# A causal layer's inverse products, split by token halves over two row halves of TensorE's array

## The chip, the cores and the metric

The kernel runs on one core of a Trainium2 chip. The metric is the device time of one execution in microseconds; the time given for a kernel is the median of its runs. A profiled execution gives, beside its own time, the trace: every instruction on the five engines (PE is TensorE with PEld its weight loads, DVE is VectorE, ACT is ScalarE, POOL is GpSimd, SP is SyncE, which issues DMAs), with its start, its duration and what it waited for.

## The reference

A model of four layers over x of 4 sequences x 512 tokens x 128 channels: a state space layer, an attention block with routed experts, a causal layer, and the attention block again. The change lies in the third, the causal layer:

```python
probs = jax.nn.softmax(logits + causal_mask, axis=-1)      # 16 heads of 8 channels, rotary q and k
L = jnp.eye(s, dtype=probs.dtype) - jnp.tril(probs, -1)
rhs = jnp.diagonal(probs, axis1=-2, axis2=-1)[..., None] * v
A = jax.scipy.linalg.solve_triangular(L, rhs, lower=True)
attn_output = A.transpose(0, 2, 1, 3).reshape(b, s, HID)
return attn_output @ Wd.T + bd
```

So each token's row is its own probability times v plus a weighted sum of the solved rows of all earlier tokens: a triangular solve for each head.

## The kernel before

`delta_phase` computes the causal layer. Tokens go in 16 tiles of 128 (4 a sequence, `n` counts them), and each tile in 8 blocks of 16 tokens (`BLK`, `BLKS`). E is the matrix of exponentials of a tile's own scores, kept for each head in `e_nat` (tokens x earlier tokens); `xT` holds, for each head, the inverses of the eight 16 x 16 diagonal blocks, scaled by the row sums, and zeros elsewhere. POOL makes the inverses (`inverse_block`), and SyncE brings them into place by DMA (`inverses`).

`multiplied` on TensorE makes the inverse products: for every head one matmul with `e_nat` as the stationary and `xT` as the moving operand, 128 x 128 x 128 in f32, four heads in one PSUM bank (L2560), and `multiplied` on ScalarE copies the bank of 128 x 512 into `mT` (L2146). There are four such groups a tile, at the hooks 9, 10, 11 and 12 (`MT_HOOKS`) of the tile before. PSUM has eight banks: two for step sums (`STEP`), two for transposes (`TURN`), two that ScalarE empties (`TO_ACT`) and two that VectorE empties (`TO_DVE`). Uses of `TO_ACT` are numbered in program order by `act_use`; they alternate between the two banks, and `act_free` makes TensorE wait until the use two before has been copied out.

The solve of a tile then takes 7 steps (k = 1 to 7, `TURNS` is the last), for two halves of 8 heads that take turns. A half step is: `product` on TensorE (L2601), for 8 heads, two rounds of four heads side by side in strips of 32 columns, with `a_nat`'s first 16k tokens as the stationary operand and 16 columns of `mT` as the moving one; an addition by VectorE into `aT` (L2430); `turned` on TensorE, a transpose of all 128 tokens of `aT` (`turn_half`, L2606), where `aT` is the stationary operand and the identity the moving one; a copy by ScalarE into `a_nat`, or after the last step into `a_all` (`turned`, L2183). Steps 1 to 7 of both halves make 14 hooks, and `beside(n, h)` puts other tiles' work between them, in an order written out by hand: maxima of tile n+4 or n+3, scores of n+3 (`score`), sums and their transposes of n+2, inverse products of n+1. At a tile's start come the products with earlier tiles (`from_earlier`), transposes of `gT`, and the first product with `xT` (`inverse`). Every engine runs its own queue in program order.

Of the kernel before, what the change touches and what calls it, by code (L numbers as in the profile page):

```python
# [19 lines left out]
P = 128  # L20
# [1707 lines left out]
def delta_phase(core, nc):  # L1728
# [4 lines left out]
    with ExitStack() as ctx:  # L1733
# [64 lines left out]
        def shift_in(n):  # L1798
            return s["m_in_odd" if n % 2 else "m_in_even"]

        def later_tiles(n):
            b, t = bt(n)
            return b * (TPB - 1) + t
# [10 lines left out]
        def own_cols(t, half):  # L1814

            n = NH // 2 * HEAD_COLS
            pairs = t[:, half * n:(half + 1) * n + 2 * HD].rearrange("p (g r) -> p g r", g=2)
            return pairs[:, :, 0:n // 2].rearrange("p g (h c) -> p g h c", h=GROUP)[:, :, :, 0:HD]
# [7 lines left out]
        def turn_bank(half):  # L1826
            return ps[:, TURN[half], 0:P]

        def turned_cols(half):
            return turn_bank(half).rearrange("p (h c) -> p h c", h=GROUP)[:, :, 0:2 * HD].rearrange(  # L1830
                "p h (g d) -> p g h d", g=2)

        def in_program(n):
# [62 lines left out]
        def act_use(kind, n, i=0):  # L1896
            act_place[kind, n, i] = len(act_place)
# [4 lines left out]
        for n in range(-LEAD, TILES_N):  # L1902
            if n >= 1:
                dve_use("output", n - 1)
            for h in range(HOOKS):
                if in_program(n + 2) and (n + 2) % TPB and h == 2:
                    dve_use("turned_sums", n + 2)
                if starts_in(n, 4) is not None and h == 6:
                    dve_use("own", starts_in(n, 4))
                if maxima_done(n, h) is not None:  # L1910
                    dve_use("turned_maxima", maxima_done(n, h))
                for m, hd in maxima_in(n, h):
                    dve_use("maximum", m, hd)
                if starts_in(n, LEAD) is not None and h == 13:
                    dve_use("values", starts_in(n, LEAD))
                if begins_early(n + 1) and h == 13:
                    dve_use("first_tiles", n + 1)
                for i in scores_in(n, h):
                    act_use("score", n + 3, i)
                if in_program(n + 1) and h in MT_HOOKS:  # L1920
                    act_use("mt", n + 1, MT_HOOKS.index(h))
                if in_program(n + 2) and (n + 2) % TPB and h == 0:
                    act_use("sums", n + 2)
                if in_program(n + 2) and h == 3:
                    act_use("column", n + 2)
                if goes_on(n, LEAD) is not None and h == 12:
                    act_use("hT", goes_on(n, LEAD))
                if goes_on(n, 5) is not None and h in (0, 1):
                    act_use("qk", goes_on(n, 5), h)
        dve_use("output", TILES_N - 1)  # L1930

        def in_act(kind, n, i=0):
            return act_place[kind, n, i] + 1
# [4 lines left out]
        def act_bank(kind, n, i=0):  # L1938
            return ps[:, TO_ACT[act_place[kind, n, i] % 2], :]
# [8 lines left out]
            return in_act("score", n, DIAG_GROUPS - 1)  # L1948

        def all_mt(n):  # L1950
            return in_act("mt", n, len(MT_HOOKS) - 1)

        def all_maxima(n):
            return in_dve("maximum", n, NH // heads_at_once(n) - 1)
# [5 lines left out]
        with nc.Block() as block:  # L1960
# [129 lines left out]
            def _(act):  # L2090
# [51 lines left out]
                                             bank[:, 0:heads * t * P], ACT.Exp, scale=SCALE).then_inc(s["act_out"], 1)  # L2142

                def multiplied(n, i):
                    act.wait_ge(s["act_ps"], in_act("mt", n, i))
                    nc.scalar.copy(mT[:, n % 2, i * GROUP:(i + 1) * GROUP, :].rearrange("p h i -> p (h i)"),  # L2146
                                   act_bank("mt", n, i)).then_inc(s["act_out"], 1)

                def sums_leave(n):
                    act.wait_ge(s["act_ps"], in_act("sums", n))  # L2150
# [28 lines left out]

                def turned(n, half, k):  # L2180
                    act.wait_ge(s["an_ps"], 2 * (n * BLKS + k) + half + 1)
                    out = a_all[:, n % TPB, :] if k == TURNS else a_nat[:, :]
                    nc.scalar.copy(own_cols(out, half), turned_cols(half)).then_inc(s["an_sb"], 1)  # L2183

                act.wait_ge(s["set"], 5)
                for n in range(-LEAD, TILES_N):
# [259 lines left out]
            def _(pe):  # L2446
# [107 lines left out]
                def multiplied(n, i):  # L2554
                    if i == 0:
                        pe.wait_ge(s["x_in"], 16 * BLKS * (n + 1))
                    bank = act_free("mt", n, i)
                    for hh in range(GROUP):
                        hd = i * GROUP + hh
                        last = nc.tensor.matmul(bank[:, hh * P:(hh + 1) * P], e_nat[:, n % 3, hd, :], xT[:, n % 2, hd, :],  # L2560
                                                start=True, stop=True)
                    last.then_inc(s["act_ps"], 1)

                def head(half, gl, hh):
                    return (2 * half + gl) * GROUP + hh
# [36 lines left out]
                                                    of_head(lhs[rows, :], hd), rhs(hd), start=(gl == 0), stop=(gl == 1))  # L2602
                    last.then_inc(done, 1)

                def turn_half(half, src, done):
                    nc.tensor.transpose(turn_bank(half), src[:, half, :], core.ident[:, :]).then_inc(done, 1)  # L2606

                def output(n):
                    bank = dve_free("output", n)
# [37 lines left out]
                def turned(n, half, k):  # L2647
                    pe.wait_ge(s["at_sb"], 2 * (n * BLKS + k) + half + 1)
                    if n >= 1 and k == 0:
                        pe.wait_ge(s["an_sb"], 2 * BLKS * n - 1 + half)  # L2650
                    turn_half(half, aT[:, n % 2], s["an_ps"])

                pe.wait_ge(s["set"], 5)
                for n in range(-LEAD, TILES_N):
# [114 lines left out]
```

## Time and profile before

| | us |
|---|---|
| median of three runs (lowest, highest) | 1573.53 (1573.26, 1580.44) |
| the profiled execution | 1573.51 |
| its span, first to last instruction | 1571.7 |
| TensorE busy | 1268.3 (81%) |
| VectorE busy | 996.3 (63%) |
| ScalarE busy | 726.2 (46%) |
| GpSimd busy | 626.5 (40%) |
| mean granted clock of TensorE | 0.849 |

Busy time counts an engine's instructions; a share of the whole span mixes layers with different limits, so it has to be read stage by stage. TensorE's granted clock is given as a share of 2.4 GHz: it stands either at 1.00 (2.4 GHz) or at 0.50 (1.2 GHz), and a mean in between is a mixture of both.

### The profile page before, as it was taken

Reading aid. Unit: us, or ns where it says so; the run is one execution under the profiler, and the core shown is the slowest. Engines: PE = TensorE matmul, PEld = TensorE weight load, DVE = VectorE, ACT = ScalarE, POOL = GpSimd, SP = SyncE. Lnnn points to the kernel's source line nnn. Section 1 sums busy time; section 2 is a strip of 40 time slices with the busy share of each in tenths; the row PEclk is TensorE's granted clock in tenths of the full one; section 3 lists DMA queues with packets and bytes.
Section 4 is the critical chain, followed back from the end, with each engine's and each line's share of the span. In section 5 each row is a group of like instructions: output and inputs, shape, how many; then the busy total and the mean of one; then the engine's idle time right before and its main releaser. Section 6 shows DMA issues by size and latency. Waiting matters only on the chain. (4 is left out here: it accounts for less than half of the span.)

```text
span 1571.7 us, 30564 instructions
## 1 busy us (share of the span) xinstructions
PE 1268.3 (81%) x11629; PEld 698.6 (44%) x11658; DVE 996.3 (63%) x2122; ACT 726.2 (46%) x1578; POOL 626.5 (40%) x838
## 2 busy tenths in 40 slices
PE   7857677689999949237889999988989799999765
PEld 3323233233333329124766666666666223333365
DVE  3699999788879435336546646645522777887143
ACT  3833344217777827113524523623442057777543
POOL 1388898653241225203423333333231712522143
PEclk9988888869999979656779879978977579999878
DMA  4379742131431102131331231141120333140122
GB/s 136 147 255 377 266 155 86 49 84 34 114 75 48 69 24 62 35 81 23 64 51 28 46 68 30 34 82 19 27 38 9 79 68 70 55 110 22 56 64 76
DMA packets 127270, 126.36 MB, mean 80 GB/s; under 512 B 86802, under 2 KB 111954, under 8 KB 121525
## 3 DMA queue, kind: packets, MB, share of 16 engines
q1 hardware_dynamic: 123822, 118.28, 27.3%
q0 software_dynamic: 2496, 5.13, 1.1%
q8 instruction: 93, 1.52, 0.4%
q10 hardware_dynamic: 806, 0.99, 0.2%
q14 instruction: 53, 0.43, 0.1%
HBM read 103.56 MB, written 38.62 MB: 90 GB/s over the span
## 5 line engine op out<-in xcount | busy, mean ns | idle before, releaser
L1280 DVE TENSOR_REDUCE f_row_min<-f_ps 128x1 f32<-128x512 f32 x512 | 324.2, 679 | 73.3 <-PE f_ps L1557 69.6
L1188 ACT ACTIVATE f_e<-f_ps 128x512 f32<-128x512 f32 x512 | 280.4, 602 | 147.9 <-PE f_ps L1577 142.2
L1557 PE MATMUL f_ps<-f_operands 72*128 72x512 bf16 x512 | 212.1, 425 | 28.7 <-DMA f_operands<-k_scr 14.9
L1577 PE MATMUL f_ps<-f_operands 75*128 75x512 bf16 x512 | 190.3, 387 | 6.0 <-DMA f_operands<-m_scr 3.4
L738 PE MATMUL m_ps<-m_shared,sb_ident 128*128 128x512 f32 x256 | 137.1, 684 | 53.7 <-DVE m_shared L594 52.3
L357 POOL TENSOR_TENSOR m_drive<-m_du,m_ring 128x1024 f32<-128x1024 f32 x64 | 151.0, 2375 | 52.4 <-DVE m_ps L586 33.2
L474 ACT ACTIVATE m_ps<-m_delta,m_A 128x511 f32<-128x511 f32 x128 | 83.1, 681 | 129.3 <-DVE m_ps L586 104.7
L1588 PE MATMUL f_ps<-f_e,f_v_op 128*32 128x512 f32 x1024 | 138.2, 611 | 2.4 <-ACT f_e L1188 1.4
L2278 DVE TENSOR_REDUCE d_row_min<-d_ps 128x1 f32<-128x384 f32 (+3 forms) x176 | 106.4, 634 | 52.2 <-PE d_ps L2496 51.0
L1557 PEld LDWEIGHTS f_ps<-f_operands 72*128 72x128 bf16 x512 | 52.2, 102 | 190.3 <-DVE f_row_min L1280 136.4
L2430 DVE TENSOR_TENSOR d_aT<-d_ps,d_aT 128x16 f32<-128x16 f32 x224 | 37.9, 169 | 149.0 <-PE d_ps L2601 148.6
L738 PEld LDWEIGHTS m_ps<-m_shared,sb_ident 128*128 128x128 f32 x256 | 52.3, 215 | 140.1 <-DVE m_shared L594 82.1
L2183 ACT COPY d_a_nat<-d_ps 128x64 f32<-128x64 f32 x224 | 47.8, 213 | 125.9 <-PE d_ps L2606 124.6
L586 DVE TENSOR_TENSOR_SCAN m_ps<-m_ps,m_drive 128x1024 f32<-128x1024 f32 x44 | 101.1, 2297 | 5.2 <-POOL m_drive L357 0.2
L2606 PE MATMUL d_ps<-sb_ident,d_aT 128*128 128x128 f32 x256 | 88.5, 349 | 13.4 <-DVE d_aT L2430 10.9
L2493 PE MATMUL d_ps<-d_k_op,d_q_op 72*128 72x128 bf16 (+3 forms) x256 | 72.9, 356 | 31.6 <-DMA d_k_op<-k_scr 20.1
L1982 POOL TENSOR_TENSOR d_xT_blk<-d_e_blk,d_zi_blk 128x256 f32<-128x256 f32 x16 | 13.3, 830 | 210.6 <-DVE d_zi_blk L2339 210.6
L2560 PE MATMUL d_ps<-d_xT,d_e_nat 128*128 128x128 f32 x512 | 90.2, 334 | 3.3 <-DMA d_xT<-x_scr 1.9
L1066 POOL DMA_INDIRECT f_rows_scr<-f_h2n,f_place_u x32 | 32.7, 1022 | 147.7 <-DVE f_place_u L1404 140.4
L2560 PEld LDWEIGHTS d_ps<-d_xT,d_e_nat 128*128 128x128 f32 x512 | 82.7, 245 | 6.1 <-issue 3.1
L2601 PE MATMUL d_ps<-d_mT,d_a_nat 32*32 32x16 f32 (+6 forms) x3584 | 76.6, 194 | 8.7 <-ACT d_a_nat L2183 6.2
L1577 PEld LDWEIGHTS f_ps<-f_operands 75*128 75x128 bf16 x512 | 49.3, 100 | 64.5 <-ACT f_e L1188 33.1
(270 smaller groups left out, 2337.7 us busy)
## 6 DMA issues: line engine op xcount, KB each, us to landing
m_ring<-bc_scr SPq DMA_DIRECT2D x32, 1024.0 KB, 6.8
f_rows_scr<-blank SPq DMA_DIRECT2D x2, 8707.5 KB, 32.8
f_wall<-f_wall SPq DMA_DIRECT2D x16, 578.0 KB
f_operands<-q_scr SPq DMA_DIRECT2D x32, 288.0 KB
f_operands<-k_scr SPq DMA_DIRECT2D x96, 96.0 KB
d_q_op<-q_scr SPq DMA_DIRECT2D x8, 576.0 KB
d_k_op<-k_scr SPq DMA_DIRECT2D x24, 192.0 KB
f_operands<-f_rows_scr SPq DMA_DIRECT2D x46, 64.5 KB, 1.8
```

The costliest lines, as they stand in the source:

```text
L357: nc.gpsimd.tensor_tensor(drive[:, step % AHEAD, :].rearrange("p (a s) -> p a s", a=HALVES), du[:, :, tokens(b)], b_row(step).unsqueeze(1) ...
L474: last = nc.scalar.activation(ps[:, at + 1:at + S], delta[:, k, b * S + 1:(b + 1) * S], ACT.Exp, scale=A[:, k, n:n + 1])
L586: nc.vector.tensor_tensor_scan(h, bank(DECAY + HALVES * (step % 2), HALVES), drive[:, step % AHEAD, :], 0.0, ALU.mult, ALU.add).then_inc(s ...
L738: last = nc.tensor.matmul(bank(Y + k), core.ident[:, :], hC[:, k * S:(k + 1) * S], start=False, stop=last_of_batch)
L1188: nc.scalar.activation(e_sb[:, n % 3, hh, :], ps[:, SCORE[(b * UNITS + u) % SCORE_BANKS], :], ACT.Exp, scale=SCALE).then_inc(s["e_out"], 1)
L1280: nc.vector.tensor_reduce(row_min[:, b % 2, u // TPB, u % TPB:u % TPB + 1], ps[:, MAXQ[(b * UNITS + u) % MAX_BANKS], :], AX.X, ALU.max, ne ...
L1557: nc.tensor.matmul(ps[:, MAXQ[n % MAX_BANKS], :], q_op(b, QK)[:, hd, t * P:(t + 1) * P], k_op(b, QK)[:, hd, :], start=True, stop=True).the ...
L1577: nc.tensor.matmul(ps[:, SCORE[n % SCORE_BANKS], :], k_op(b, QKS)[:, hd, t * P:(t + 1) * P], q_op(b, QKS)[:, hd, :], start=True, stop=True ...
L1588: last = nc.tensor.matmul(ps[hh * HEAD_COLS:(hh + 1) * HEAD_COLS, O_BANK, :], v_of(b, t, g * GROUP + hh), e_sb[:, n % 3, hh, :], start=(t ...
L2278: nc.vector.tensor_reduce(row_min[:, n % 2, g * heads:(g + 1) * heads], dve_bank("maximum", n, g)[:, 0:heads * cols].rearrange("p (h c) -> ...
L2560: last = nc.tensor.matmul(bank[:, hh * P:(hh + 1) * P], e_nat[:, n % 3, hd, :], xT[:, n % 2, hd, :], start=True, stop=True)
L2606: nc.tensor.transpose(turn_bank(half), src[:, half, :], core.ident[:, :]).then_inc(done, 1)
```

## The change

In `multiplied`, every head's matmul becomes two. The earlier half takes tokens 0 to 63 as contraction rows, 64 stationary columns (earlier tokens 0 to 63) and 64 moving columns; the later half takes tokens 64 to 127, 128 stationary columns and 64 moving columns. They write to two different banks, so a group of four heads now uses both banks of `TO_ACT` at once, and ScalarE copies each of them (64 x 256 and 128 x 256). The zero blocks between the halves of `xT` are no longer multiplied. The quarter of `mT` that isn't written any more (earlier tokens 64 to 127 for tokens 0 to 63) is never read. In a half step before the last, the transpose takes only `turned_rows(k)`, that is 32, 64, 96 or 128 tokens, and the copy after it only those partitions.

```diff
+        token_halves = (slice(0, P // 2), slice(P // 2, P))
...
+        def turned_rows(k):
+
+            return slice(0, (k // 2 + 1) * 2 * BLK)
...
                 if in_program(n + 1) and h in MT_HOOKS:
-                    act_use("mt", n + 1, MT_HOOKS.index(h))
+                    act_use("mt", n + 1, 2 * MT_HOOKS.index(h))
+                    act_use("mt", n + 1, 2 * MT_HOOKS.index(h) + 1)
...
         def all_mt(n):
-            return in_act("mt", n, len(MT_HOOKS) - 1)
+            return in_act("mt", n, 2 * len(MT_HOOKS) - 1)
...
                 def multiplied(n, i):
-                    act.wait_ge(s["act_ps"], in_act("mt", n, i))
-                    nc.scalar.copy(mT[:, n % 2, i * GROUP:(i + 1) * GROUP, :].rearrange("p h i -> p (h i)"),
-                                   act_bank("mt", n, i)).then_inc(s["act_out"], 1)
+                    heads = slice(i * GROUP, (i + 1) * GROUP)
+                    for half, tokens in enumerate(token_halves):
+                        earlier = slice(0, tokens.stop)
+                        act.wait_ge(s["act_ps"], in_act("mt", n, 2 * i + half))
+                        nc.scalar.copy(mT[earlier, n % 2, heads, tokens],
+                                       act_bank("mt", n, 2 * i + half)[earlier, 0:GROUP * P // 2].rearrange(
+                                           "p (h i) -> p h i", h=GROUP)).then_inc(s["act_out"], 1)
...
                 def turned(n, half, k):
                     act.wait_ge(s["an_ps"], 2 * (n * BLKS + k) + half + 1)
-                    out = a_all[:, n % TPB, :] if k == TURNS else a_nat[:, :]
-                    nc.scalar.copy(own_cols(out, half), turned_cols(half)).then_inc(s["an_sb"], 1)
+                    out, rows = (a_all[:, n % TPB, :], slice(0, P)) if k == TURNS else (a_nat[:, :], turned_rows(k))
+                    nc.scalar.copy(own_cols(out[rows], half), turned_cols(half, rows)).then_inc(s["an_sb"], 1)
...
-                    bank = act_free("mt", n, i)
+                    banks = [act_free("mt", n, 2 * i + half) for half in range(2)]
                     for hh in range(GROUP):
                         hd = i * GROUP + hh
-                        last = nc.tensor.matmul(bank[:, hh * P:(hh + 1) * P], e_nat[:, n % 3, hd, :], xT[:, n % 2, hd, :],
-                                                start=True, stop=True)
-                    last.then_inc(s["act_ps"], 1)
+                        for half, tokens in enumerate(token_halves):
+                            earlier = slice(0, tokens.stop)
+                            last = nc.tensor.matmul(banks[half][earlier, hh * P // 2:(hh + 1) * P // 2],
+                                                    e_nat[tokens, n % 3, hd, earlier], xT[tokens, n % 2, hd, tokens],
+                                                    start=True, stop=True)
+                            if hh == GROUP - 1:
+                                last.then_inc(s["act_ps"], 1)
...
-                def turn_half(half, src, done):
-                    nc.tensor.transpose(turn_bank(half), src[:, half, :], core.ident[:, :]).then_inc(done, 1)
+                def turn_half(half, src, done, tokens=slice(0, P)):
+                    nc.tensor.transpose(turn_bank(half)[tokens], src[:, half, tokens], core.ident[:, :]).then_inc(done, 1)
...
-                    turn_half(half, aT[:, n % 2], s["an_ps"])
+                    turn_half(half, aT[:, n % 2], s["an_ps"], slice(0, P) if k == TURNS else turned_rows(k))
```

## Rows read from the trace of the kernel before

**Rows 1.** Windows, causal layer: length, PE, PEld, DVE, ACT, POOL busy, clock, DMA.

```profile
734.00:1217.00 483.00, 432.24 (x7554) 317.88 (x7582) 244.11 (x740) 193.22 (x545) 153.46 (x473) 0.85 0.23 41
```

**Rows 2.** Waits, 760 to 1217: us in total, times, longest.

```profile
DVE d_aT L2430 <- PE d_ps L2601: 146.9, 114, 8.1
...
PE d_ps L2606 <- DVE d_aT L2430: 10.6, 22, 2.1
```

**Rows 3.** Groups by form; then single lines, ns min/median/max: L2560 and L2606.

```profile
L2560 PE MATMUL d_ps<-d_xT,d_e_nat 128*128 128x128 f32 x512 | 90.2, 334 | 3.3 <-DMA d_xT<-x_scr 1.9 <-ACT d_e_off L2141 1.4
...
L2560 PEld LDWEIGHTS d_ps<-d_xT,d_e_nat x512: 186/192/392, 749.4 to 1201.3; 128*128 128x128 f32 x171
L2560 PE MATMUL d_ps<-d_xT,d_e_nat x512: 274/275/582, 749.5 to 1201.4; 128*128 128x128 f32 x171
...
L2606 PE MATMUL d_ps<-sb_ident,d_aT x256: 270/328/477, 757.7 to 1217.6; 128*128 128x128 f32 x128
```

**Rows 4.** Timeline, PE, high clock: start, us from first start to last end.

```profile
874.15 0.27 PE L2501 MATMUL d_ps<-sb_ident,d_row_min 128*16 128x128 f32 x1
874.26 1.06 PE L2560 MATMUL d_ps<-d_xT,d_e_nat 128*128 128x128 f32 x8
875.15 0.27 PE L2606 MATMUL d_ps<-sb_ident,d_aT 128*128 128x128 f32 x1
...
875.60 1.16 PE L2560 MATMUL d_ps<-d_xT,d_e_nat 128*128 128x128 f32 x8
876.69 0.32 PE L2601 MATMUL d_ps<-d_mT,d_a_nat 112*32 112x16 f32 x16
...
877.11 1.06 PE L2560 MATMUL d_ps<-d_xT,d_e_nat 128*128 128x128 f32 x8
```

**Rows 5.** L2601, strips of 32 columns: durations in ns, min/median/max.

```profile
L2601 PEld LDWEIGHTS d_ps<-d_mT,d_a_nat x3584: 101/109/159, 758.4 to 1217.1; 16*32 16x32 f32 x29, 48*32 48x32 f32 x29, 80*32 80x32 f32 x29, 112*32 112x32 f32 x29
L2601 PE MATMUL d_ps<-d_mT,d_a_nat x3584: 177/183/237, 758.4 to 1217.1; 16*32 16x16 f32 x29, 48*32 48x16 f32 x29, 80*32 80x16 f32 x29, 112*32 112x16 f32 x29
L2601 PEld LDWEIGHTS d_ps<-d_xT,d_g_nat x512: 106/110/110, 756.6 to 1206.5; 128*32 128x32 f32 x171
```

**Rows 6.** Timeline of weight loads in the first layer; then L693's own durations.

```profile
46.47 0.19 PEld L675 LDWEIGHTS m_ps<-m_shared,sb_m_W 128*128 128x128 f32 x1 [0.24 <-issue]
46.90 0.19 PEld L675 LDWEIGHTS m_ps<-m_shared,sb_m_W 128*128 128x128 f32 x1 [0.24 <-issue]
47.85 0.29 PEld L693 LDWEIGHTS m_ps<-m_shared,sb_m_dt 64*128 64x128 f32 x2 [0.76 <-issue]
...
L693 PEld LDWEIGHTS m_ps<-m_shared,sb_m_dt x16: 182/185/187, 34.0 to 67.4; 64*128 64x128 f32 x16
```

**Rows 7.** Timeline, PE, a stretch that begins at the low clock.

```profile
934.19 1.98 PE L2560 MATMUL d_ps<-d_xT,d_e_nat 128*128 128x128 f32 x8
...
937.13 0.63 PE L2516 MATMUL d_ps<-d_k_op,d_q_op 75*128 75x128 bf16 x4 [0.22 <-issue]
937.56 1.84 PE L2560 MATMUL d_ps<-d_xT,d_e_nat 128*128 128x128 f32 x8
```

**Rows 8.** ScalarE: timeline, then single lines with ns min/median/max.

```profile
878.20 0.59 ACT L2146 COPY d_mT<-d_ps 128x512 f32<-128x512 f32 x1 [0.68 <-PE d_ps L2560]
...
L2183 ACT COPY d_a_nat<-d_ps x224: 203/213/225, 758.0 to 1216.6; 128x64 f32<-128x64 f32 x112
...
L2136 ACT ACTIVATE d_e_nat<-d_ps x64: 589/597/598, 705.5 to 1136.2; 128x512 f32<-128x512 f32 x64
```

**Rows 9.** Windows around a tile's four groups (three of sixteen), clock third from last.

```profile
749.50:755.70 6.20, 6.20 (x35) 6.12 (x33) 4.98 (x14) 1.87 (x4) 4.87 (x18) 0.58 0.01 2
...
872.70:878.00 5.30, 5.30 (x87) 4.79 (x85) 4.33 (x15) 2.26 (x7) 4.13 (x16) 1.00 0.02 4
...
1194.40:1201.50 7.10, 7.01 (x83) 6.41 (x84) 0.53 (x3) 2.22 (x6) 0.00 (x0) 0.71 0.01 2
```

**Rows 10.** Windows, the stretch right behind such groups.

```profile
907.70:911.00 3.30, 2.85 (x67) 1.87 (x69) 1.80 (x6) 0.91 (x3) 0.68 (x2) 1.00 0.80 195
```

More of the change, by code:

```diff
@@ L1827, in turn_bank, with turned_cols @@
             return ps[:, TURN[half], 0:P]
-        def turned_cols(half):
-            return turn_bank(half).rearrange("p (h c) -> p h c", h=GROUP)[:, :, 0:2 * HD].rearrange(
+        def turned_rows(k):
+            return slice(0, (k // 2 + 1) * 2 * BLK)
+        def turned_cols(half, rows=slice(0, P)):
+            return turn_bank(half)[rows].rearrange("p (h c) -> p h c", h=GROUP)[:, :, 0:2 * HD].rearrange(
                 "p h (g d) -> p g h d", g=2)
```

## The prediction

> **What bounds the kernel now.** I read the page first, for the stage the diff touches: the causal layer lies between about 734 and 1217 us. The windows view of it [rows 1] shows TensorE busy in 432 of 483 us, VectorE in 244, ScalarE in 193, at a granted clock of 0.85. The waits there [rows 2] say the same: VectorE waits 146.9 us for the strip products, TensorE 10.6 us for VectorE. So in this stage TensorE's time is the layer's time, and only what lies between its instructions can hide anything. The execution profiled took 1573.51 us around a span of 1571.7; the median of the runs is 1573.53, so the sum can be made against either.
>
> **The inverse products (L2560).** 64 groups of four heads, each matmul in two passes, so 8 loads and 8 streams a group, 90.2 us in all [rows 3]. In the order of time [rows 4] a group of 8 takes 1.06 us from first start to last end. One matmul lasts 0.275 [rows 3], so the pitch is (1.06-0.275)/7 = 0.112 us. What makes that pitch? Loads: 128 f32 columns last 192 ns, 32 columns 110 [rows 3, 5], 0.85 ns a column, so 128 columns are 0.109 us of loading. Streams: 128 columns 275 ns, 16 columns 183 [rows 3, 5], 0.82 ns a column, so 0.105. Load and stream both fill the pitch. The change halves the streamed columns but not this load: the later half still loads 128 columns (keys 0 to 127), the earlier one 64. Fewer rows make no load shorter: those of 16 to 112 rows share one range, 101 to 159 ns, and 64 rows by 128 columns take 185 [rows 5, 6]. So a group holds 8 loads of 128 and 8 of 64 columns where it held 8 of 128. Even if the halves run side by side, the 8 long loads alone are 0.89 us, today's time. The best case inside a group is no gain.
>
> The bad case is the shape. The halves are a 64 x 64 and a 64 x 128 corner of the array, and they alternate. Where the kernel now goes from one division of the array to another it pays: from full matmuls to products of 32-column strips, the group's last start is 874.26+1.06-0.275 = 875.045 and full transposes follow at 875.15 (0.105 later, no wait), but after the group at 875.60 the strips follow at 876.69, which is 0.205 after the last start 876.485 [rows 4]. The same with 64 rows, read on the loads: those of a run of full 512-column matmuls start 0.43 apart (46.47, 46.90), each one matmul ahead; the first 64-row load starts at 47.85, behind the last full matmul, 0.95 later and so 0.09 more than two pitches [rows 6]. So a change of division costs about 0.093 us and the lost cover of the load. No row shows 64 x 64 next to 64 x 128. Bounds: zero (they count as one division, or disjoint rows don't matter) and 0.093 at every change. I take the upper end, since both neighbours that change a row or a column division pay it.
>
> The Trainium skill's TensorEngine Tiling (Key Properties) states that changing the tiling mode, not just the tile, drains the engine, and it lists 64x64 and 64x128 as separate modes; the rows above agree for the pairs they show, and by that rule the upper end holds. TensorE: Matmul & The Clock Gate (Part 3) says against it that tiles in different row groups run together, four of them at 3.07 times the speed; no row here shows row tiles side by side, and by that rule the lower end would hold.
>
> The sum of a pair at the upper end: later half, two loads 0.22, stream of 64 columns 0.053, wait 0.093: 0.37. Earlier half 0.058+0.058+0.053+0.093 = 0.26. Four heads: 2.52 us, against 0.89. At the low clock (1.2 GHz) a group takes 1.98 us [rows 7], about 1.7 without its tail; loads and streams double and so does part of the wait: 4.5. How many groups are low: 90.2 = 1.1 x 42 + 2.0 x 22. So 42 x 1.63 + 22 x 2.8 = +130 us. Entering the group adds a change where scores or transposes now run straight in: 0.093 plus 0.05 of uncovered load, x 64 = +10.
>
> **ScalarE and the banks.** A copy of 512 columns is 586 ns, of 64 columns 213 [rows 8], so 256 columns cost 0.373 and the pair 0.746: +0.16 x 64 = 10 us on an engine with 290 idle in the stage, no price by itself. But each group now needs both banks free. In order of time the copy starts 0.03 after the group's end (877.11+1.06 = 878.17, copy at 878.20) [rows 4, 8], and the next group starts 0.28 after (875.32 to 875.60). With both copies due, about 0.78, TensorE would wait 0.5, with a transpose and a strip product queued behind it, whose sums VectorE waits for. If halves are drained one after the other, the earlier half's copy runs inside the last pair and this wait is nearly nil; if they run together it costs some 17 us over the 48 gaps (those at the low clock are longer). In both cases nine groups follow a score group in their own hook (L2516 then L2560, 937.13 to 937.56 [rows 7]) and must wait for its exponential, 0.6 us [rows 8], and four follow the last off-diagonal scores: +10.
>
> **The transposes (L2606).** The stationary operand narrows from 128 to 32, 64 or 96 columns; the identity still streams 128. A transpose with its load uncovered lasts 328 ns, covered 270 [rows 3, 4]: 0.055 for 128 columns. Per half the steps save 96+96+64+64+32+32 = 384 columns, 0.165 us; x 32 = 5.3, less the covered ones: -4. ScalarE's copies have fewer partitions and the same columns: nothing. A transpose of 16 columns between full ones (874.15 to 874.26 [rows 4]) pays no change of division, so I add none.
>
> Not read any more: the stale rows of mT and a_nat, since step k reads rows below 16k. The semaphore counts move with the doubled uses and nothing waits longer for that. SyncE's wait for all of a tile's groups (before the inverses two tiles on) has a tile's time in hand. Zero.
>
> **The clock.** This is the term I can size least. The mean granted clock of the 16 stretches that hold a tile's four groups is under 0.8 in twelve [rows 9], and in the 3 us behind each of the twelve it is 1.00 (one of the twelve: [rows 10]). So the clock rises in these groups: back-to-back 128-column streams after a stretch of small products. The change takes them away, and at the upper end leaves TensorE streaming in a quarter of the time there. If the clock then stays low through all groups, the 42 fast ones cost 4.5 and not 2.52 (+84), and about 5 us behind each of 16 tiles runs low at a loss of about 0.4 per us (a group is 1.06 at one clock and 1.98 at the other [rows 4, 7]; small products lose less): +32. Bounds 0 and +116. I take somewhat over half, +70, since four of the sixteen stretches stand at 1.00 throughout, held there by what runs before them (one of the four: [rows 9]).
>
> **Sum.** +130 +10 +10 -4 +70 = +216, so 1790 us. With the clock as it is now: 1720. With all of it: 1836, and more if it stays low elsewhere.
>
> **Rivals.**
> 1. The halves run together and no change is paid between them. Then the group keeps its 0.89, plus entries 10, own-hook waits 10, bank waits 17, transposes -4: +33, 1607. The low clock adds up to 42 x 0.8 + 32 = 66, since each matmul streams half as much: to 1675. Nothing runs together but no wait either gives (0.112+0.058) x 8 = 1.36 us a group, +40 in all, in the same span. For it: strip products of four heads run together now (16 in 0.32 us [rows 4]). Against it: the unequal corners. Center 1640. Chance 0.30.
> 2. Faster: the pair is set by its 64-column streams alone, pitch 0.056, if the loads of the row halves overlap and cost less than columns say. Then -0.45 x 42 - 0.9 x 22 = -39, and with +10 +10 -4 and ScalarE's copies falling inside neighbouring work: -23, 1550. It decides below a pair pitch of about 0.08. Against it: 64-row loads of 128 columns take 185 ns [rows 6]. Chance 0.04.
> 3. The edits cancel: rival 1's group, bank waits hidden in idle time that TensorE has anyway (51 of 483 us), clock unchanged, transposes paying for the entries: within 0.5%. Chance 0.04.
> The forecast, changes paid at each alternation: 0.62, with its own range 1700 to 1870.
>
> **How the numbers follow.** The likeliest case gives 1790. For 8 in 10 the range must take most of rival 1 and the clock's upper bound: 1625 to 1870. Slower by over 0.5% (about what a measurement here can tell): 0.62+0.30, 0.92; same 0.04; faster 0.04.
>
> **What would show it.** Right: the starts of an L2560 group spread over about 2.5 us at the high clock, loads not ahead of the previous matmul, PE's busy time in the stage up by far more than ScalarE's. Rival 1: a group of 16 in about 1.1 us, and waits of L2560 for the mT copies of 0.4 us. Clock term: stretches behind the groups below 1.00. Transposes: uncovered loads under 110 ns at 32 columns. I am wrong altogether if the loads of the two halves start within 0.01 us of each other and a group's starts lie within 0.5 us.

## The result, and the profile after

The changed kernel took 1783.03 us (median of five runs, 1775.44 to 1790.43), 1.130 times the time of before, with a 95% interval of 1.1255 to 1.1343. Five runs of the kernel before stand beside it, with a median of 1575.59; the 1573.53 above is that of three of them. The forecast was 1790, in 1625 to 1870. The execution profiled took 1787.28 us, 213.8 over that of before.

The page of the changed kernel, the engines' busy time and then the granted clock in 40 slices (tenths of full speed):

```profile
PE 1482.9 (83%) x12141; PEld 841.0 (47%) x12170; DVE 995.8 (56%) x2122; ACT 738.7 (41%) x1642; POOL 625.9 (35%) x838
...
PEclk9889898599998865656675667567755658999978
```

TensorE has 215 us more to do, and ScalarE 12.5 for its doubled copies (10 were forecast); VectorE and GpSimd stand where they stood. The windows view of its causal layer (length, busy times of PE, PEld, DVE, ACT, POOL, clock, DMA), to be laid beside [rows 1]:

```profile
734.00:1430.00 696.00, 649.93 (x7951) 460.48 (x7979) 243.41 (x734) 204.72 (x603) 155.53 (x483) 0.66 0.16 29
```

The layer grew from 483 to 696 us, and its mean clock fell from 0.85 to 0.66. A mean of two levels gives the time at the lower one: 2 x (1 - 0.66) x 696 = 473 us at 1.2 GHz, where it was 2 x 0.15 x 483 = 145. Further down I call this the low time. (The expectations of the later runs begin at about 690 us and so count some 45 us more: 194 for before, 300 for three corners and 525 for the change are the same times as 145, 257 and 473 here.) The inverse products, in the view that groups by form (busy, mean ns, idle before), where before had the one row at the head of [rows 3]:

```profile
L2573 PE MATMUL d_ps<-d_xT,d_e_nat 64*128 64x64 f32 x512 | 172.9, 439 | 0.0
L2573 PE MATMUL d_ps<-d_xT,d_e_nat 64*64 64x64 f32 x512 | 118.8, 333 | 11.5 <-ACT d_e_nat L2143 7.2 <-ACT d_e_off L2148 2.9 <-ACT d_mT L2156 1.3
```

Both forms together (they overlap a little) are busy for 260.3 us by the page; it was 90.2. One group at the high clock and one at the low one, TensorE in order of time:

```profile
1243.17 0.22 PE L2507 MATMUL d_ps<-sb_mask_up,sb_ident_b 128*128 128x128 bf16 x1
1243.32 2.54 PE L2573 MATMUL d_ps<-d_xT,d_e_nat 64*64 64x64 f32 x16
1245.79 0.32 PE L2616 MATMUL d_ps<-d_mT,d_a_nat 96*32 96x16 f32 x16
...
1246.62 4.13 PE L2573 MATMUL d_ps<-d_xT,d_e_nat 64*64 64x64 f32 x16
1250.68 0.47 PE L2621 MATMUL d_ps<-sb_ident,d_aT 128*128 128x128 f32 x1
```

16 passes take 2.54 us where 8 took 1.06 [rows 4]; at the low clock 4.1 where it was 1.98 [rows 7] (the group shown is no exception: all 59 groups that ran low throughout took 4.09 to 4.13). Why, the weight loads of the first group show:

```profile
1243.32 0.19 PEld L2573 LDWEIGHTS d_ps<-d_xT,d_e_nat 64*64 64x64 f32 x2 [0.21 <-issue]
...
1243.58 0.29 PEld L2573 LDWEIGHTS d_ps<-d_xT,d_e_nat 64*128 64x128 f32 x2
...
1243.94 0.13 PEld L2573 LDWEIGHTS d_ps<-d_xT,d_e_nat 64*64 64x64 f32 x1
```

Two loads of the earlier half, then nothing until 1243.58, then two of the later half, then nothing until 1243.94. In this group no load runs ahead across a change of half, and 0.62 us go by for a head: 0.26 for the earlier half and 0.36 for the later one. The low clock does the rest: of the 64 groups one ran at the high clock throughout, and four more began there. Windows around a tile's four groups (three tiles of sixteen; the third is the one with the highest clock), and then two short stretches behind the third:

```profile
794.50:812.80 18.30, 18.22 (x115) 13.81 (x115) 1.21 (x4) 3.15 (x10) 6.17 (x20) 0.50 0.71 138
...
885.30:904.00 18.70, 18.70 (x118) 13.92 (x116) 5.15 (x19) 3.33 (x11) 8.48 (x25) 0.50 0.15 26
1243.30:1260.10 16.80, 16.80 (x118) 12.56 (x116) 5.62 (x19) 3.27 (x11) 8.21 (x27) 0.58 0.15 26
...
1260.10:1263.10 3.00, 3.00 (x51) 2.45 (x54) 0.77 (x2) 1.30 (x4) 0.00 (x0) 0.50 0.36 33
1266.00:1269.00 3.00, 2.76 (x55) 2.01 (x57) 1.21 (x5) 0.40 (x2) 0.00 (x0) 1.00 0.00 0
```

Before, such stretches took 5 to 9 us, and the clock stood at 1.00 behind twelve of them [rows 9, 10]. Now fifteen of the sixteen stand at 0.54 or less, and the 3 us behind them as well, though TensorE counts as busy nearly all the time, and even a stretch that begins at the high clock (the third) ends low.

### The profile page after: what moved, and what is told of

Same layout as the page of the kernel before. It is cut to its first block and busy times, and to the rows that moved or that the text cites. A ratio compares the mean times of both kernels' runs of the same rounds, so it can differ in the third digit from the quotient of the medians.

```text
span 1785.4 us, 31700 instructions
## 1 busy us (share of the span) xinstructions
PE 1482.9 (83%) x12141; PEld 841.0 (47%) x12170; DVE 995.8 (56%) x2122; ACT 738.7 (41%) x1642; POOL 625.9 (35%) x838
## 5 line engine op out<-in xcount | busy, mean ns | idle before, releaser
L2573 PE MATMUL d_ps<-d_xT,d_e_nat 64*64 64x64 f32 (+1 forms) x1024 | 260.3, 386 | 11.5 <-ACT d_e_nat L2143 7.2
L2573 PEld LDWEIGHTS d_ps<-d_xT,d_e_nat 64*64 64x64 f32 (+1 forms) x1024 | 196.8, 250 | 77.0 <-ACT d_e_nat L2143 9.3
L2156 ACT COPY d_mT<-d_ps 64x256 f32<-64x256 f32 (+1 forms) x128 | 47.3, 369 | 243.1 <-PE d_ps L2573 243.1
L2621 PE MATMUL d_ps<-sb_ident,d_aT 128*32 128x128 f32 (+3 forms) x256 | 93.8, 368 | 11.9 <-DVE d_aT L2441 8.8
L2194 ACT COPY d_a_nat<-d_ps 32x64 f32<-32x64 f32 (+3 forms) x224 | 46.0, 205 | 133.9 <-PE d_ps L2621 132.7
L2504 PE MATMUL d_ps<-d_k_op,d_q_op 72*128 72x128 bf16 (+3 forms) x256 | 72.0, 349 | 25.9 <-DMA d_k_op<-k_scr 20.0
L2616 PE MATMUL d_ps<-d_mT,d_a_nat 32*32 32x16 f32 (+6 forms) x3584 | 80.6, 200 | 6.7 <-ACT d_a_nat L2194 6.2
```

The lines of the kernel that those rows point to most:

```text
L2573: last = nc.tensor.matmul(banks[half][earlier, hh * P // 2:(hh + 1) * P // 2], e_nat[tokens, n % 3, hd, earlier], xT[tokens, n % 2, hd, to ...
L2621: nc.tensor.transpose(turn_bank(half)[tokens], src[:, half, tokens], core.ident[:, :]).then_inc(done, 1)
```

## The experiments

All times are set against runs of the kernel before on the same chip. Two theories were to be told apart first. Division: TensorE waits, and can't load ahead, whenever the size of the corner it works in changes, and the two halves have unlike corners. Count and size: more and smaller matmuls and loads cost more, whatever their corners. A third question was how much of the loss is the clock's.

**The transposes alone.** The kernel before with `turned_rows` and nothing else of the change:

```diff
-                    nc.scalar.copy(own_cols(out, half), turned_cols(half)).then_inc(s["an_sb"], 1)
...
+                    nc.scalar.copy(own_cols(out[rows], half), turned_cols(half, rows)).then_inc(s["an_sb"], 1)
...
-                    turn_half(half, aT[:, n % 2], s["an_ps"])
+                    turn_half(half, aT[:, n % 2], s["an_ps"], slice(0, P) if k == TURNS else turned_rows(k))
```

> The kernel before with the narrowed transposes and their copies alone; the inverse products are as before. Both theories (the slowdown comes from changes of the array's division; it comes from more and smaller matmuls and loads) put all of it on the inverse products, so this run should not be slower: 5 us less by the load time saved (384 columns a half and tile at 0.43 ns), 1565 to 1575. If a 32 or 64 column transpose counts as a division of its own, its 160 narrowed neighbours would cost 0.1 each and the time would be 1585 to 1600.

Measured: 1576.62 us, ratio 0.999 (0.9961 to 1.0019). Not to be told from no change, and the 4 us I gave it lie inside the interval. So the whole loss is with the inverse products, and narrowed transposes between full matmuls cost no wait: in this run's trace they start 0.06 us behind a full bf16 matmul (874.18, then the transpose of 64 columns at 874.24), as those of 128 columns did before.

**Halves one after the other.** The same 16 passes, sorted:

```diff
-                    for hh in range(GROUP):
...
-                        for half, tokens in enumerate(token_halves):
...
+                    for half, tokens in enumerate(token_halves):
+                        earlier = slice(0, tokens.stop)
+                        for hh in range(GROUP):
...
```

> The changed kernel with the loops swapped: four matmuls of the earlier half, then four of the later half, so the same 16 passes change the division once inside a group and not seven times. If changes of division cost it (0.09 to 0.15 us each plus the load's lost cover): a group 1.4 to 1.6 us at the high clock and about 2.8 at the low one, not 2.3 and 3.7; 64 x 1.0 = 65 us less, 1690 to 1725, and down to 1660 if the clock holds in some groups. If the number and size of matmuls cost it: no difference, 1775 to 1790.

Measured: 1717.29 us, ratio 1.0895 (1.0836 to 1.0954). A group at the high clock, TensorE in order of time:

```profile
910.85 1.71 PE L2573 MATMUL d_ps<-d_xT,d_e_nat 64*64 64x64 f32 x16
912.49 0.32 PE L2615 MATMUL d_ps<-d_mT,d_a_nat 96*32 96x16 f32 x16
```

1.71 us and not 2.54 (the expectation counts from first to last start, which is 0.2 less), with the same loads and streams and six changes fewer: 0.14 us for a change with its lost cover. Count and size would have left it as it was. 66 us of the loss are this order alone.

**Equal corners.** The earlier half also takes 128 stationary columns, so both are 64 x 128:

```diff
-                            earlier = slice(0, tokens.stop)
-                            last = nc.tensor.matmul(banks[half][earlier, hh * P // 2:(hh + 1) * P // 2],
-                                                    e_nat[tokens, n % 3, hd, earlier], xT[tokens, n % 2, hd, tokens],
+                            last = nc.tensor.matmul(banks[half][:, hh * P // 2:(hh + 1) * P // 2],
+                                                    e_nat[tokens, n % 3, hd, :], xT[tokens, n % 2, hd, tokens],
```

> The changed kernel with both halves as 64 rows x 128 columns (the earlier half too takes all 128 stationary columns), alternating as before. One division throughout, unlike corners gone. Division theory: no wait inside a group. If row halves of one division also run together, a pair takes one pitch of 0.11 at the high clock, a group 0.9 to 1.1, and the time is 1600 to 1660; if they take turns, 16 loads of 128 columns are 1.8 us at the high clock and 3.5 at the low one, 1720 to 1770. Count-and-size theory: more load columns than the change, so 1800 or above.

Measured: 1652.15 us, ratio 1.0465 (1.0411 to 1.0518). In order of time:

```profile
1049.36 1.11 PE L2572 MATMUL d_ps<-d_xT,d_e_nat 64*128 64x64 f32 x16
1050.39 0.32 PE L2615 MATMUL d_ps<-d_mT,d_a_nat 96*32 96x16 f32 x16
```

Its windows view, and its inverse products by form:

```profile
734.00:1306.00 572.00, 524.59 (x8109) 378.54 (x8108) 245.55 (x743) 196.27 (x610) 153.02 (x474) 0.69 0.19 35
```

```profile
L2572 PE MATMUL d_ps<-d_xT,d_e_nat 64*128 64x64 f32 x1024 | 119.7, 406 | 14.7 <-ACT d_e_nat L2143 7.2 <-ACT d_mT L2156 3.5 <-ACT d_e_off L2148 2.9
```

More work than in the change, in less than half the time: 16 passes in 1.11 us, what 8 full ones take [rows 4]. Row halves of one size run side by side, and the pair goes at the pitch of one load of 128 columns, 0.11. This is what the change was written for and didn't get, since its corners are unlike. It also shows the forecast's point that the load holds the group: with halves side by side and half the streams, a group is no shorter than before.

The kernel is still 4.7% slower than before, and the group's length isn't the reason: at the high clock it is what it was. The low time is: 2 x 0.31 x 572 = 355 us, where before had 145. So equal corners take away 131 us of the change's loss, and some 75 remain without any unlike corners.

**Three equal corners.** The later half is cut in two, so that each head has three matmuls of 64 x 64:

```diff
-                        for half, tokens in enumerate(token_halves):
-                            earlier = slice(0, tokens.stop)
+                        for half, cols in ((0, 0), (1, 0), (1, 1)):
+                            tokens, earlier = token_halves[half], token_halves[cols]
...
-                            if hh == GROUP - 1:
+                            if hh == GROUP - 1 and half == cols:
```

> The changed kernel with the later half cut in two, so that every head has three matmuls of 64 rows x 64 columns x 64 moving columns, in three corners of the array, all of one division. Division theory with corners running together: a round of three takes 0.06 us at the high clock, a group of 24 passes about 0.5, and with entry, exit and the bank waits the time is 1560 to 1620. If corners take turns: 24 x 0.058 = 1.4 us a group at the high clock, 2.6 at the low one, 1660 to 1700. Count-and-size theory: half as many matmuls again, 1800 or above.

Measured: 1596.93 us, ratio 1.0109 (1.0055 to 1.0162). A group at the high clock and two at the low one:

```profile
882.76 0.69 PE L2573 MATMUL d_ps<-d_xT,d_e_nat 64*64 64x64 f32 x24
884.25 0.69 PE L2573 MATMUL d_ps<-d_xT,d_e_nat 64*64 64x64 f32 x24 [0.20 <-ACT d_mT L2156]
...
815.50 1.13 PE L2573 MATMUL d_ps<-d_xT,d_e_nat 64*64 64x64 f32 x24
819.04 1.12 PE L2573 MATMUL d_ps<-d_xT,d_e_nat 64*64 64x64 f32 x24 [0.84 <-ACT d_e_nat L2143]
```

24 passes in 0.69 us: the group is now well under the 1.06 of before, and its 64 groups are busy for 63.7 us in all, 26 less than before. Yet the kernel is 1% slower than before. The windows view shows what it pays with:

```profile
734.00:1248.00 514.00, 456.34 (x8625) 313.37 (x8625) 245.15 (x743) 195.76 (x610) 154.03 (x478) 0.75 0.21 39
```

The low time is 2 x 0.25 x 514 = 257 us where it was 145.

**Whole rows.** Two matmuls a head, 128 x 128 both, 64 moving columns each; banks and copies as in the change:

```diff
-                            earlier = slice(0, tokens.stop)
-                            last = nc.tensor.matmul(banks[half][earlier, hh * P // 2:(hh + 1) * P // 2],
-                                                    e_nat[tokens, n % 3, hd, earlier], xT[tokens, n % 2, hd, tokens],
+                            last = nc.tensor.matmul(banks[half][:, hh * P // 2:(hh + 1) * P // 2],
+                                                    e_nat[:, n % 3, hd, :], xT[:, n % 2, hd, tokens],
```

> The changed kernel with every head's two matmuls over all 128 rows and 128 stationary columns, 64 moving columns each, still in two banks and with two copies. No change of division anywhere in the group or at its ends; twice the loads of before. If the load sets the pitch (0.112 for 128 columns, whatever streams), a group takes 15 x 0.112 = 1.68 us from first to last start at the high clock and about 3.2 at the low one; if the stream does, 0.9. With the load theory and the clock as before: 1573 + 64 x 0.9 + 15 for the banks = 1645; with the clock low in the groups because only half of the columns stream: 1720 to 1760. If the stream sets the pitch: 1585 to 1600.

Measured: 1712.72 us, ratio 1.0843 (1.0771 to 1.0914). In order of time:

```profile
920.53 1.95 PE L2572 MATMUL d_ps<-d_xT,d_e_nat 128*128 128x64 f32 x16
```

Twice the loads with half the stream each, no change of division: (1.95 - 0.27)/15 = 0.112 a pass, the old pitch. The load of 128 columns sets it. The time lies between the two forecasts of the load theory, 1645 with the clock as before and 1720 or more with it low: the layer takes 621 us at a mean clock of 0.73, 335 us of low time.

**The clock: dense work put back.** The three-corner kernel with the four full matmuls of before ahead of each group, their result overwritten:

```diff
                     banks = [act_free("mt", n, 2 * i + half) for half in range(2)]
+                    for hh in range(GROUP):
+                        nc.tensor.matmul(banks[1][:, 0:P], e_nat[:, n % 3, i * GROUP + hh, :],
+                                         xT[:, n % 2, i * GROUP + hh, :], start=True, stop=True)
```

> The three-corner kernel (1597 us) with four full 128 x 128 x 128 f32 matmuls ahead of each group, the very ones of the kernel before, their result overwritten: extra work of 0.9 us at the high clock in each of 64 groups, 58 us, or 105 if the clock stays low. Clock theory (the groups of before raised the clock for themselves and what follows, and lighter groups don't): the low time of the layer falls from 300 us to under 200 as before, the fill gives back some 40 us, and the time is 1600 to 1630. If the clock doesn't depend on these groups: 1655 to 1700 with as much low time as before.

Measured: 1640.20 us, ratio 1.037 (1.0306 to 1.0435). Its windows view and its two groups of inverse products by form, the fill first:

```profile
734.00:1290.00 556.00, 489.08 (x9145) 355.32 (x9146) 249.19 (x750) 194.63 (x611) 157.16 (x489) 0.87 0.21 37
```

```profile
L2570 PE MATMUL d_ps<-d_xT,d_e_nat 128*128 128x128 f32 x512 | 89.9, 331 | 19.9 <-ACT d_mT L2156 9.2 <-ACT d_e_nat L2143 7.2 <-ACT d_e_off L2148 2.9
L2576 PE MATMUL d_ps<-d_xT,d_e_nat 64*64 64x64 f32 x1536 | 51.6, 249 | 0.0
```

The fill is busy for 90 us and costs 43. The time is 10 us above the dearest that the clock theory gave and 15 below the cheapest without it; the low time decides between them. It is back at 2 x 0.13 x 556 = 145 us, and the mean granted clock of the whole program is 0.854 to 0.861 in all four runs, where the three-corner kernel had 0.823 to 0.827. What a microsecond at the low clock costs can be estimated outside these groups. There the layer took 514 - 64 = 450 us without the fill and 556 - 137 = 419 with it (137 is the busy time of both kinds together, which overlap a little). Of the low time, 255 and 150 us by the clock's own records, 52 and 58 lie in the groups, so 203 and 92 outside: 31 us for 111, or 0.28 us for each. The 41 runs of the kernel before that stand beside the experiments agree: a line through them gives 0.27 us of time for each us of low time in the whole program (450 to 521 us).

**The clock: dense work taken from the kernel before.** Three of four heads' inverse products are left out and bf16 identity matmuls stand for them:

```diff
-                        last = nc.tensor.matmul(bank[:, hh * P:(hh + 1) * P], e_nat[:, n % 3, hd, :], xT[:, n % 2, hd, :],
-                                                start=True, stop=True)
+                        made = (e_nat[:, n % 3, hd, :], xT[:, n % 2, hd, :]) if hh == 0 else (w["ident_b"], w["ident_b"])
+                        last = nc.tensor.matmul(bank[:, hh * P:(hh + 1) * P], *made, start=True, stop=True)
```

> The kernel before with three of the four heads' inverse products of each group left out: bf16 identity matmuls of one pass stand in their place, banks, copies and waits unchanged. TensorE's work falls by 0.5 us a group at the high clock and 1.0 at the low one, 43 us over the 42 high and 22 low ones. If the clock doesn't hang on these groups: 1530 to 1540, low time no longer than before (194 us). Clock theory: the low time grows by 60 to 120 us at a price of some 0.4 per us, so that more than half of the gain is lost: 1555 to 1590.

Measured: 1573.65 us where before had 1581.95 beside it, ratio 0.9944 (0.9913 to 0.9975). Its windows view:

```profile
734.00:1215.00 481.00, 428.77 (x7410) 300.82 (x7410) 244.00 (x743) 194.84 (x547) 155.02 (x478) 0.78 0.23 42
```

At the clock of before, 43 us of work were taken away, and 8 us came back; in the profiled executions the layer is 2 us shorter, 481 against 483. The low time went from 145 to 2 x 0.22 x 481 = 212. One execution's low time varies, but all ten runs of this kernel have a mean granted clock of 0.818 to 0.835, and all thirteen of the kernel before beside it one of 0.836 to 0.856. The groups are busy for 60 us instead of 90, and outside them the layer took 481 - 60 = 421 us instead of 393, for 159 us of low time there instead of 100: 0.48 us for each, so this price lies between 0.28 and 0.48. Only TensorE's work in these groups was changed, so in the kernel before, too, they carry the clock of the layer.

**Order within a hook.** The three-corner kernel with the products ahead of the same hook's scores, on TensorE, on ScalarE and in `act_use`:

```diff
+                    if in_program(n + 1) and h in MT_HOOKS:
+                        multiplied(n + 1, MT_HOOKS.index(h))
                     for i in scores_in(n, h):
                         score(n + 3, i)
...
-                    if in_program(n + 1) and h in MT_HOOKS:
-                        multiplied(n + 1, MT_HOOKS.index(h))
```

> The three-corner kernel with the inverse products put ahead of the scores of the same hook, on TensorE and on ScalarE and in the numbering of the banks' uses. The thirteen groups that had to wait for an exponential of their own hook (9.3 + 2.9 us in the waits of the three-corner kernel) no longer wait for it just issued: 5 to 12 us less than 1597, 1585 to 1592. If those waits lay beside other idle time: no difference, 1593 to 1600.

Measured: 1603.36 us, ratio 1.0134 (1.0074 to 1.0193): no gain; the expected 5 to 12 us didn't come. Its waits show where they went. The wait for the exponential fell from 9.3 to 1.9 us, and the scores (L2524, L2536) now wait for the mT copies instead (us, times, longest):

```profile
PE d_ps L2524 <- ACT d_mT L2156: 4.0, 9, 0.5
PEld d_ps L2524 <- ACT d_mT L2156: 3.6, 6, 0.6
PEld d_ps L2536 <- ACT d_mT L2156: 2.4, 4, 0.6
...
PEld d_ps L2573 <- ACT d_e_nat L2143: 1.9, 6, 0.4
```

**The fill in the changed kernel.** The same four matmuls ahead of each group of the changed kernel:

```diff
+                    for hh in range(GROUP):
+                        nc.tensor.matmul(banks[1][:, 0:P], e_nat[:, n % 3, i * GROUP + hh, :],
+                                         xT[:, n % 2, i * GROUP + hh, :], start=True, stop=True)
```

> The changed kernel with the four full matmuls of before run ahead of each group and overwritten: 0.9 us of extra dense work a group at the high clock (58 us in all), as in the three-corner kernel with the fill. Clock theory: part of the groups, all but one of which ran at 3.7 us at the low clock, now run at 2.3 at the high one; the low time of 525 us falls by 100 to 250 and the fill comes nearly free: 1770 to 1810. If the groups themselves drop the clock again whatever runs ahead of them, or the clock doesn't hang on it: 1840 to 1890 with the low time unchanged or longer.

Measured: 1878.91 us, ratio 1.1902 (1.1842 to 1.1963). The expectation of the clock theory failed. Its windows view:

```profile
734.00:1527.00 793.00, 743.34 (x8603) 551.03 (x8630) 247.13 (x743) 205.72 (x611) 153.21 (x480) 0.68 0.14 25
```

Twelve groups, not one, ran high, but the low time stayed at 2 x 0.32 x 793 = 508 us, and the fill cost 96 us. Dense work ahead doesn't carry the clock through groups whose matmuls wait for each other; in this run it was low in 52 of 64.

**A bank of each pair.** The three-corner kernel, with the earlier halves in a bank of `TO_DVE`, copied by VectorE:

```diff
-                    banks = [act_free("mt", n, 2 * i + half) for half in range(2)]
+                    banks = [dve_free("mt", n, i), act_free("mt", n, i)]
...
+                def multiplied(n, i):
+                    heads, tokens = slice(i * GROUP, (i + 1) * GROUP), token_halves[0]
+                    dve.wait_ge(s["dve_ps"], in_dve("mt", n, i))
+                    nc.vector.tensor_copy(mT[tokens, n % 2, heads, tokens],
+                                          dve_bank("mt", n, i)[tokens, 0:GROUP * P // 2].rearrange(
+                                              "p (h i) -> p h i", h=GROUP)).then_inc(s["dve_out"], 1)
...
-                                last.then_inc(s["act_ps"], 1)
+                                last.then_inc(s["act_ps" if half else "dve_ps"], 1)
```

> The three-corner kernel (1597 us) with the earlier halves' products in one of VectorE's banks and copied by VectorE, the later halves' in one of ScalarE's as before, so that each group takes one bank of each pair and both pairs alternate again. If the waits for the mT copies and for the exponentials of the same hook (9.1 + 9.3 + 2.9 us of the loads' waits in the three-corner kernel) are on TensorE's path: 15 to 25 us less, 1572 to 1582. If low clock is what bounds those stretches, and the waits are refilled by later ones: 1585 to 1600.

Measured: 1595.04 us, ratio 1.0101 (1.0052 to 1.0149): the same as without. The waits of the three-corner kernel, and then of this one:

```profile
PEld d_ps L2504 <- DVE d_row_min L2289: 11.7, 31, 1.3
...
PEld d_ps L2573 <- ACT d_e_nat L2143: 9.3, 9, 1.1
PEld d_ps L2573 <- ACT d_mT L2156: 9.1, 26, 0.5
...
PE d_ps L2573 <- ACT d_e_nat L2143: 7.2, 9, 0.8
...
PE d_ps L2504 <- DVE d_row_min L2289: 3.0, 7, 1.2
PE d_ps L2573 <- ACT d_e_off L2148: 2.9, 4, 0.7
PE d_ps L2573 <- ACT d_mT L2156: 2.9, 12, 0.3
```

```profile
PEld d_ps L2512 <- DVE d_row_min L2288: 25.0, 32, 4.9
...
PE d_ps L2512 <- DVE d_row_min L2288: 15.7, 10, 4.6
...
PEld d_ps L2581 <- DVE d_mT L2295: 5.2, 20, 0.4
```

The matmuls of the groups stood idle for ScalarE for 7.2 + 2.9 + 2.9 = 13.0 us, and 1.4 are left of it. The maxima (L2504, here L2512) now wait for VectorE's minima instead: 3.0 us of TensorE's idle time became 15.7. That the one replaced the other is plain from these rows; why isn't shown. The maxima may have been due to wait all along (the kernel before has 7.9 us of this wait), or they wait because VectorE has 64 copies more to do. No version that computes the whole layer beats the kernel before; the transposes alone stand level with it.

## Why the prediction was right, point by point

- **A change of division at every half: right, and the size close.** The step gave 0.37 + 0.26 = 0.63 us a head at the high clock; the loads show 0.36 + 0.26. The group gave 2.52; it is 2.54, and its starts spread over 2.3. That unlike corners on disjoint rows are two divisions was the open choice between bounds; the order of the halves and the equal corners settle it. The Trainium skill's TensorEngine Tiling (Key Properties) states that changing the tiling mode, not just the tile, drains the engine, and the trace agrees; that this holds between unlike sizes on disjoint rows too is what the runs add (0.62 us a head against 0.28 with equal corners).
- **The load sets the pitch: right.** Whole rows kept 0.112 a pass, equal corners 1.11 us a group.
- **The low clock's group: too dear.** I gave 4.5; 4.1 was measured. I had let loads and waits grow with the clock more than they do. The count beneath it was rough as well: where I took 42 groups of before as high and 22 as low, the trace has 36 high throughout, 19 low and 9 in which the clock changed.
- **The clock: right mechanism, too small.** "I take somewhat over half" of the 116 us failed: not half but all groups but one went low. The high clock that four of the sixteen stretches had before didn't last through groups that bring it down themselves. Outside the groups the price of 0.4 a us lies within what the runs give, but the time was too short: 80 us, where some 117 were added. The misses, a group too dear and too few low groups, largely cancel: with its share of the 70, the forecast had some +180 us in the groups, where 260 - 90 = +170 was measured, and +35 outside them, where it was +43. That 1790 lies within 7 us of the time owes something to luck.
- **ScalarE's two banks: right in size, and not the bound.** In the changed kernel 13 groups wait for an exponential of their hook (7.2 + 2.9 us by form, forecast 10), and those for the copies are short, as forecast for halves drained in turn. Where such waits were taken away, in the three-corner kernel, nothing came back; in the changed kernel it wasn't tried.
- **The transposes: not measurable.** -4 us forecast, -0.4% to +0.2% measured.
- **The other rivals.** Rival 1's mechanism exists, in the kernel with equal corners, at 1652 in its span of 1607 to 1675, but it isn't this change. Rival 2's pitch exists as well, in three corners (0.69 us a group), and it isn't faster: outside its groups the layer took 57 us more than before, with 103 us more of low time.

The sum from the two profiles: groups at the high clock 64 x 2.54 = 163 us against 64 x 1.08 = 69 makes +94; the low clock within them 260 - 163 = 97 against 90 - 69 = 21 makes +76; the rest of the layer 696 - 260 = 436 against 483 - 90 = 393 makes +43. Together 213, as measured (the stretch after ends 6 us before the layer's last transpose, and in that execution the rest of the program was 5 us shorter). The rest of the layer has about 117 us more of low time (473 less 256 in groups, against 145 less 45). At 0.28 to 0.48 each these are 33 to 56 us, so the clock can account for all of the +43, and the forecast's +10 for entering the groups and +10 for waits in the same hook can't be told apart from it. So of the loss some 94 us are the waits between unlike corners at the high clock, and up to 119 come with the low clock; the share of the rest is an estimate.

Equal corners cut the loss the other way, by an experiment: 131 us go with the unlike corners (the 94, and what the same waits cost more at the low clock), and 75 stay. Outside its groups that kernel takes 572 - 120 = 452 us against 393, and has some 240 us of low time there, where the change has 217. So the clock is lost with equal corners too.

## What to carry to other kernels

If a matmul is split over parts of TensorE's array, cut it into parts of one size: here equal parts ran side by side (64 x 128 twice, 64 x 64 three times), and unlike ones took turns with a wait each. Look first at whether the weight load or the stream sets the pitch: where the load does, as here, halving the stream gains nothing. And before making dense matmuls lighter, read the granted clock through and behind them: they may be what holds it up for everything that follows.

## What the runs showed of the hardware

- Weight loads of plain f32 matmuls go by columns: 0.85 ns each at 2.4 GHz, whatever the rows, and a matmul of 64 moving columns behind a load of 128 goes at 0.112 us.
- Three corners of 64 x 64 run 24 f32 passes in 0.69 us, and two row halves of 64 x 128 run 16 in 1.11.
- A change between a 64 x 64 and a 64 x 128 corner on disjoint rows costs about 0.14 us, wait and lost cover together. A transpose of 32, 64 or 96 columns between full matmuls isn't such a change (0.06 us behind a full bf16 matmul, like one of 128).
- TensorE can be busy by every record of a stretch (18.70 of 18.70 us at 885.30) and be granted 0.50 all through it.
- Four full f32 matmuls a group more, or three fewer, move the granted clock of a whole layer: with them back in front of three equal corners its low time fell from 257 to 145 us; with three of four taken from the kernel before it rose from 145 to 212.
- A us at the low clock outside these groups cost 0.28 to 0.48 us, an estimate from those two pairs of runs.
